# One attention kernel: the slope added by accumulating DMAs, the bar in one instruction, the mask in halves

## The chip, the cores and the metric

The kernel runs on one core of one Trainium2 chip. The metric is the device time of one execution in microseconds (us). The engines are named as the profile names them: PE (matrix multiply), PEld (its weight loads), DVE (the vector engine), ACT (the scalar engine), POOL (GpSimd) and SP (the sync engine, which issues DMAs). SBUF is the on-chip memory of 128 partitions, PSUM the memory that PE writes.

## The reference, cut to what matters

The input is 32 images of 32 channels and 56 x 56 = 3136 points. A locally connected 3 x 3 layer comes first. The part that fills most of the time is graph attention among the 3136 points of one image:

```python
p = pts / max(norm(pts, axis=1), 1e-12)
dist = sq + (-2 p @ p.T) + sq.T
_, nn_idx = top_k(-dist, 16)
nbr = pts[nn_idx]
logits = leaky_relu(cat(e, e_n) @ W_att + b_att, negative_slope=0.1)
attn = softmax(logits, axis=2)
agg = sum(nbr * attn, axis=2)
y = cat(pts, agg) @ W_conv + b_conv
```

A batch norm over y, a ReLU and a residual end it.

## The kernel before, in words

`build` (L1306) calls six stages; `attend` (L652) holds the change. It takes an image as 25 tiles of 128 query points (TILES), 800 tiles in all, and never gathers neighbours: it scores each query against all 3136 points, sets the logits of points outside the top 16 far below the rest, takes the exponential of all of them and sums with a matrix product.

Each engine runs its own stream; `each_step` (L638) calls a `body` for every step, in which `tile(0)` is the step's tile, `tile(-1)` the next one and `tile(1)` the one before. The order of calls in a body is the order on that engine; semaphores join the streams. The first and last steps are written out, and 50 steps (two images) are the body of a loop. What one tile goes through:

- PE `score` (L863): two halves of 1568 scores into PSUM. ACT `copy_scores` (L985, copy at L990) brings each half to `scores`, which has two buffers; the copy of quad 0 waits until the mask of the tile two steps back has read that buffer.
- ACT `rise` (L977, L982) writes the upper part of the leaky ReLU, relu(0.9 x logit) up to a factor, into `masked`, a ring of five buffers.
- POOL `add_slope` (L833, L843) adds the lower part, the slope (`shares`, one row for each image, in all partitions), to the first 1568 columns of `masked`, in two instructions of 784 columns. It is called for `tile(0)`, after the bar of `tile(1)`; the second instruction waits for the count of `tile(0)`.
- DVE `search` (L1084, L1088): the 8 largest of each 224 scores, 14 instructions. `merge` (L1144): from these the 16th largest, in a chain of six small instructions of which each waits on the semaphore `chain` for the one before (L1149 to L1159); the last, the count (L1159), raises `doubt_ready`.
- PE `add_doubts` (L878, L882) sums the counts, and DVE `settle_doubts` (L1096) loads the sum. If it isn't zero, five long instructions (L1102 to L1109) search the tile again.
- DVE `bar` (L1115): scores less the bound, capped at 0, for the first 1568 columns (L1118); the other 1568 are capped at `shares` instead (L1119), so the slope of these columns comes in here.
- DVE `mask` (L1122, L1127), one step later: adds `scores` to `masked`, and takes the smallest of the negated sums, in one instruction over 3136 columns. It raises `masked_ready`.
- ACT `exponentiate` (L1000, L1002): the exponential of `masked` and its total.
- PE `turn` (L884, L896 and L898) transposes `masked` in 25 blocks through two PSUM banks, ACT `copy_turned` (L1011, L1017) brings them back in 7 copies, and PE `aggregate` (L909, L916) multiplies. DVE `invert_total` (L1130) and `normalise` (L1134) scale the result, and a last product makes y.

SP's stream loads a batch's points, scores' second halves and shares ahead (`next_batch`, L791, in the step of tile 7 of the batch before), and loads and stores 64 KB pieces every fourth step. POOL's stream in `attend` is `add_slope` alone.

Of the kernel before, what the change touches and what calls it, by code (L numbers as in the profile page):

```python
# [5 lines left out]
FP32 = mybir.dt.float32  # L6
# [645 lines left out]
def attend(nc, feat, unit, pieces, share, table, W_emb, b_emb, W_att, b_att, W_conv, b_conv, y):  # L652
# [11 lines left out]
    POOL_COLS = N // 2  # L664
# [12 lines left out]
    with ExitStack() as stack:  # L677
# [14 lines left out]
        weight8 = enter(nc.sbuf_tensor("weight8", [P, PARTS, H8], FP32))  # L692
        best = enter(nc.sbuf_tensor("best", [P, NEIGHBOURS], FP32))
# [34 lines left out]
        logits_ready = enter(nc.semaphore("a_logits"))  # L728
# [3 lines left out]
        barred = enter(nc.semaphore("a_barred"))  # L732
        masked_ready = enter(nc.semaphore("a_masked"))
# [13 lines left out]
        y_stored1 = enter(nc.semaphore("a_y_stored1"))  # L747
        sp_passed = enter(nc.semaphore("a_sp_passed"))
# [5 lines left out]
        batch_in, feat_in, y_stored = [batch0, batch1], [feat0, feat1], [y_stored0, y_stored1]  # L754

# [71 lines left out]
        @block.gpsimd  # L827
        def _(pool):
            pool.wait_ge(cleared, 6)
            nc.gpsimd.affine_select(out=ident[:], in_=ident[:], compare_op=ALU.not_equal, fill=1.0, base=0,  # L830
                                    pattern=[[-1, P]], channel_multiplier=1).then_inc(ident_ready, 1)

            def add_slope(t, passed):  # L833

                pool.wait_ge(rises_ready, t.count(1, 1))
                if passed is not None:
                    pool.wait_ge(barred, passed.count(1, 1))
                width = POOL_COLS // 2
                for k in range(2):
                    if k == 1:  # L840
                        pool.wait_ge(doubt_ready, t.count(1, 1))
                    m = masked[:, t.ring, k * width:(k + 1) * width]
                    nc.gpsimd.tensor_tensor(m, m, shares[:, t.half, k * width:(k + 1) * width], ALU.add).then_inc(logits_ready, 1)  # L843

            def body(tile):
                if tile(0):
                    add_slope(tile(0), tile(1))

            each_step(pool, body)
# [113 lines left out]
        def _(act):  # L963
# [21 lines left out]
            def copy_scores(t, quad, used):  # L985

                act.wait_ge(scored, t.count(SCORED, SCORED_FREE + PER * (quad + 1)))
                if used is not None:
                    act.wait_ge(masked_ready, used.count(1, MASKED_FREE + 1))
                nc.scalar.activation(scores[:, t.par, quad * QUAD:(quad + 1) * QUAD].rearrange("p (a b) -> p a b", b=SCH),  # L990
                                     ps[:, 0:PER * BANK].rearrange("p (a b) -> p a b", b=BANK)[:, :, 0:SCH],
                                     ACT.Copy).then_inc(scores_in, 1)
# [27 lines left out]
            def body(tile):  # L1020
# [16 lines left out]
                if coming:  # L1037
                    copy_scores(coming, 1, None)
# [12 lines left out]
        def _(dve):  # L1051
# [63 lines left out]
            def bar(t):  # L1115

                low, high = scores[:, t.par, 0:POOL_COLS], scores[:, t.par, POOL_COLS:N]
                step(nc.vector.tensor_scalar(low, low, bound[:, 0:1], 0.0, ALU.subtract, ALU.min))  # L1118
                nc.vector.scalar_tensor_tensor(high, high, bound[:, 0:1], shares[:, t.half, POOL_COLS:N],  # L1119
                                               ALU.subtract, ALU.min).then_inc(barred, 1)  # L1120

            def mask(t):  # L1122

                gate(dve, logits_ready, t.count(2, 2), dve_passed)
                gate(dve, barred, t.count(1, 1), dve_passed)
                m = masked[:, t.ring, :]
                nc.vector.tensor_tensor_reduce(m, m, scores[:, t.par, :], -1.0, -NEVER, ALU.add, ALU.min,  # L1127
                                               minus_top[:, t.ring:t.ring + 1]).then_inc(masked_ready, 1)
# [15 lines left out]
            def merge(t, n):  # L1144

                found_all = found[:, t.par, :, :].rearrange("p a b -> p (a b)")
                last = best[:, NEIGHBOURS - 1:NEIGHBOURS]
                dve.wait_ge(chain, n)
                n = step(nc.vector.max(best[:, 0:H8], found_all))  # L1149
                dve.wait_ge(chain, n)  # L1150
                n = step(nc.vector.match_replace(rest[:], best[:, 0:H8], found_all, NEVER))
                dve.wait_ge(chain, n)
                n = step(nc.vector.max(best[:, H8:NEIGHBOURS], rest[:]))
                dve.wait_ge(chain, n)
                n = step(nc.vector.scalar_tensor_tensor(bound_low[:], over[:], last, margin[:], ALU.mult, ALU.subtract))
                dve.wait_ge(chain, n)
                n = step(nc.vector.scalar_tensor_tensor(bound[:], under[:], last, bound_low[:], ALU.mult, ALU.min))
# [187 lines left out]
```

## Time and profile before

| | |
|---|---|
| median of 3 runs | 11979.92 us (11979.1 to 11986.17) |
| span of the profiled execution | 11977.8 us, 2.1 us under that median |
| `attend`, tile by tile | from about 1.5 ms to 11.85 ms of the span |
| busy share of the span | DVE 86%, ACT 85%, PE 74%, POOL 27% |

The page of the profile gives the profiled execution's span and no other time of its own, so durations are set against the span. The span is the time from the first to the last instruction. A busy share is a mean over the whole span, so it mixes stages; views with a window show one stage. A group of instructions has one source line; its row gives its count, its busy time, the mean of one, and the idle time of its engine just before it with what ended it. "issue" is time in which an engine waited for nothing that the profile shows.

### The profile page before, as it was taken

The page shows a single profiled execution, that of the slowest core. Times are in us where ns is not written, and L with a number is a line of the kernel's source. Part 1 is how long each engine was busy: PE and PEld are TensorE (multiplying, and loading weights), DVE is VectorE, ACT ScalarE, POOL GpSimd, SP SyncE. Part 2 cuts the span into 40 slices and gives each one's busy share as a digit, 9 for nine tenths or more (in the row PEclk, how much of TensorE's full clock was granted, in tenths as well). Part 3 has the DMA queues.
Part 4 walks back from the last instruction along what each step waited for, and adds up shares of the span by engine and source line. Part 5 has one row for each costly group of instructions (what it writes and reads, how often), then busy time and mean ns, then how long its engine had stood idle before and what let it go on. Part 6 is the DMA issues. An engine that isn't in the chain of part 4 may idle for free. (4 is left out here: it accounts for less than half of the span.)

```text
span 11977.8 us, 322272 instructions
## 1 busy us (share of the span) xinstructions
PE 8919.8 (74%) x114746; PEld 6368.8 (53%) x114746; DVE 10276.0 (86%) x23897; ACT 10163.3 (85%) x11576; POOL 3199.6 (27%) x2040
## 2 busy tenths in 40 slices
PE   2885667777777777877777777777777777777775
PEld 2664345555555555555555555555555555545553
DVE  1000599999999999999999999999999999999997
ACT  2332489999999999999999998999999999989986
POOL 0221022222222222222222222222222222222221
PEclk9887889999999999999999999999999999999998
DMA  9666800000000000000000000000000000000003
GB/s 164 172 177 175 256 16 17 17 17 16 17 17 17 17 17 16 5 17 17 17 17 16 17 17 16 16 17 16 17 17 4 17 17 17 17 16 16 17 4 132
DMA packets 267542, 480.57 MB, mean 40 GB/s; under 512 B 196964, under 2 KB 197348, under 8 KB 248356
## 3 DMA queue, kind: packets, MB, share of 16 engines
q1 hardware_dynamic: 242532, 349.99, 12.5%
q0 software_dynamic: 23424, 109.21, 2.9%
q8 instruction: 1022, 16.74, 0.6%
q14 instruction: 564, 4.62, 0.1%
HBM read 353.59 MB, written 105.50 MB: 38 GB/s over the span
## 5 line engine op out<-in xcount | busy, mean ns | idle before, releaser
L843 POOL TENSOR_TENSOR masked<-masked,shares_a 128x784 f32<-128x784 f32 x1600 | 2988.8, 1868 | 7371.9 <-DVE rest L1159 4237.3
L1088 DVE MAX8 found<-scores 128x8 f32<-128x224 f32 x11200 | 3479.0, 370 | 223.7 <-ACT scores L990 188.9
L1017 ACT ACTIVATE turned_sb<-psum 128x512 f32<-128x512 f32 (+1 forms) x5600 | 2945.5, 572 | 507.7 <-PE psum L896 431.4
L898 PE MATMUL psum<-ident_a,masked 128*128 128x128 f32 x19200 | 2649.4, 282 | 902.8 <-ACT turned_sb L1017 860.9
L898 PEld LDWEIGHTS psum<-ident_a,masked 128*128 128x128 f32 x19200 | 2373.5, 195 | 1359.9 <-issue 1359.5
L1127 DVE CUSTOM_DVE_ANT_0 masked<-masked,scores 128x3136 f32<-128x3136 f32 x800 | 2719.1, 3399 | 0.2 <-DVE scores L1119 0.2
L990 ACT ACTIVATE scores<-psum 128x1568 f32<-128x1568 f32 x1600 | 2375.1, 1484 | 224.7 <-DVE minus_top L1127 190.0
L1002 ACT ACTIVATE masked<-masked,minus_top 128x3136 f32<-128x3136 f32 x800 | 2363.5, 2954 | 0.0
L982 ACT ACTIVATE masked<-shares_a,own 128x3136 f32<-128x3136 f32 x800 | 2328.4, 2910 | 1.0
L896 PE MATMUL psum<-ident_a,masked 128*128 128x128 f32 (+1 forms) x10400 | 1764.5, 284 | 528.7 <-ACT turned_sb L1017 494.1
L896 PEld LDWEIGHTS psum<-ident_a,masked 128*128 128x128 f32 (+1 forms) x10400 | 1106.7, 139 | 1289.1 <-issue 1213.3
L871 PE MATMUL psum<-points 32*128 32x392 f32 x12800 | 1542.1, 552 | 28.3 <-DMA rows<-table 16.4
L916 PE MATMUL psum<-turned_sb,rows 128*32 128x128 f32 (+1 forms) x40000 | 1554.9, 284 | 0.5 <-ACT inverse_sb L998 0.5
L1119 DVE SCALAR_TENSOR_TENSOR scores<-scores,bound,shares_a 128x1568 f32<-128x1568 f32 x800 | 1467.5, 1834 | 0.0
L916 PEld LDWEIGHTS psum<-turned_sb,rows 128*32 128x32 f32 (+1 forms) x40000 | 1159.1, 113 | 274.0 <-issue 176.5
L295 ACT ACTIVATE w_turned<-w_ps 96x384 f32<-96x384 f32 x784 | 347.2, 486 | 592.0 <-PE w_ps L254 588.4
L882 PE MATMUL psum<-ones,above 128*1 128x1 f32 x1600 | 150.8, 163 | 924.5 <-DVE rest L1159 924.5
L307 DVE COPY conv_sb<-conv_ps 128x128 f32 x196 | 57.1, 291 | 900.9 <-PE conv_ps L276 900.9
L1118 DVE TENSOR_SCALAR scores<-scores,bound 128x1568 f32<-128x1568 f32 x800 | 807.8, 1010 | 8.1 <-DVE bound L1109 2.5
L882 PEld LDWEIGHTS psum<-ones,above 128*1 128x1 f32 x1600 | 84.8, 80 | 1183.3 <-issue 1180.1
L871 PEld LDWEIGHTS psum<-points 32*128 32x128 f32 x12800 | 508.9, 186 | 229.3 <-issue 43.3
L254 PE MATMUL w_ps<-ident_c,w_in 128*96 128x128 f32 x2352 | 398.2, 312 | 232.6 <-DMA w_in<-in_L_conv_weight_dram 204.3
(137 smaller groups left out, 6415.4 us busy)
## 6 DMA issues: line engine op xcount, KB each, us to landing
w_in<-in_L_conv_weight_dram POOLq DMA_DIRECT2D x392, 144.0 KB, 3.4
w_in<-in_L_conv_weight_dram SPq DMA_DIRECT2D x392, 144.0 KB, 3.5
points<-unit SPq DMA_DIRECT2D x128, 392.0 KB
shares_a<-share SPq DMA_DIRECT2D x32, 1568.0 KB
windows<-xg SPq DMA_DIRECT2D x42, 928.0 KB, 13.5
xg<-padded SPq DMA_DIRECT2D x32, 406.0 KB, 16.8
table<-table_sb SPq DMA_DIRECT2D x32, 404.2 KB
rows<-table SPq DMA_DIRECT2D x32, 396.0 KB
```

The lines of the kernel that those rows point to most:

```text
L843: nc.gpsimd.tensor_tensor(m, m, shares[:, t.half, k * width:(k + 1) * width], ALU.add).then_inc(logits_ready, 1)
L871: nc.tensor.matmul(ps[:, r * BANK:r * BANK + SCH], points[C * r:C * (r + 1), t.half, t.queries()], points[C * r:C * (r + 1), t.half, at:at ...
L896: last = nc.tensor.transpose(out, block, ident[:])
L898: last = nc.tensor.matmul(out, block, ident[:], start=True, stop=True)
L916: last = nc.tensor.matmul(ps[q:q + C, SUM_BANK:SUM_BANK + P], rows[0:width, t.half, j, 0:C], turned_sb[0:width, t.par, j, :], start=j < PE ...
L982: nc.scalar.activation(masked[:, t.ring, :], shares[:, t.half, :], ACT.Relu, bias=own[:, t.half, at:at + 1], scale=STEEP / SLOPE).then_inc ...
L990: nc.scalar.activation(scores[:, t.par, quad * QUAD:(quad + 1) * QUAD].rearrange("p (a b) -> p a b", b=SCH), ps[:, 0:PER * BANK].rearrange ...
L1002: nc.scalar.activation(masked[:, t.ring, :], masked[:, t.ring, :], ACT.Exp, bias=minus_top[:, t.ring:t.ring + 1], scale=-1.0, accum_out=to ...
L1017: nc.scalar.activation(turned_sb[0:high, t.par, g * GROUP:g * GROUP + width // P, :].rearrange("p a b -> p (a b)"), ps[0:high, bank:bank + ...
L1088: n = step(nc.vector.max(found[:, t.par, c, :], scores[:, t.par, c * PART:(c + 1) * PART]))
L1119: nc.vector.scalar_tensor_tensor(high, high, bound[:, 0:1], shares[:, t.half, POOL_COLS:N], ALU.subtract, ALU.min).then_inc(barred, 1)
L1127: nc.vector.tensor_tensor_reduce(m, m, scores[:, t.par, :], -1.0, -NEVER, ALU.add, ALU.min, minus_top[:, t.ring:t.ring + 1]).then_inc(mask ...
```

## The change

The slope of all 3136 columns is added to `masked` by two DMAs that accumulate into SBUF, issued by GpSimd for `tile(-1)` as soon as its rise is written. The bar is then one instruction over all columns. The mask is two instructions of 1568 columns, the second starting from the first one's minimum; ACT's copy of quad 0 waits for the low half, that of quad 1 for the high half. The merge is taken apart, and its steps stand between the mask halves, `normalise` and `invert_total`.

```diff
@@ -661,7 +661,7 @@
     PART = 224
     PARTS = N // PART
     EARLY = PARTS // 2
-    POOL_COLS = N // 2
+    HALF = N // 2
     GROUP = 4
     T_GROUPS = -(-TILES // GROUP)
...
@@ -830,21 +835,16 @@
             nc.gpsimd.affine_select(out=ident[:], in_=ident[:], compare_op=ALU.not_equal, fill=1.0, base=0,
                                     pattern=[[-1, P]], channel_multiplier=1).then_inc(ident_ready, 1)
 
-            def add_slope(t, passed):
-
-                pool.wait_ge(rises_ready, t.count(1, 1))
-                if passed is not None:
-                    pool.wait_ge(barred, passed.count(1, 1))
-                width = POOL_COLS // 2
+            def add_slope(t):
+
+                gate(pool, rises_ready, t.count(1, 1), pool_passed)
                 for k in range(2):
-                    if k == 1:
-                        pool.wait_ge(doubt_ready, t.count(1, 1))
-                    m = masked[:, t.ring, k * width:(k + 1) * width]
-                    nc.gpsimd.tensor_tensor(m, m, shares[:, t.half, k * width:(k + 1) * width], ALU.add).then_inc(logits_ready, 1)
+                    cols = slice(k * HALF, (k + 1) * HALF)
+                    pool.dma_start(masked[:, t.ring, cols], shares[:, t.half, cols], accum_op=ALU.add).then_inc(slope_in[t.par], 16)
 
             def body(tile):
-                if tile(0):
-                    add_slope(tile(0), tile(1))
+                if tile(-1):
+                    add_slope(tile(-1))
 
             each_step(pool, body)
 
@@ -986,7 +986,10 @@
 
                 act.wait_ge(scored, t.count(SCORED, SCORED_FREE + PER * (quad + 1)))
                 if used is not None:
-                    act.wait_ge(masked_ready, used.count(1, MASKED_FREE + 1))
+                    if quad == 0:
+                        act.wait_ge(low_masked, used.count(1, 1))
+                    else:
+                        act.wait_ge(masked_ready, used.count(1, MASKED_FREE + 1))
                 nc.scalar.activation(scores[:, t.par, quad * QUAD:(quad + 1) * QUAD].rearrange("p (a b) -> p a b", b=SCH),
                                      ps[:, 0:PER * BANK].rearrange("p (a b) -> p a b", b=BANK)[:, :, 0:SCH],
                                      ACT.Copy).then_inc(scores_in, 1)
@@ -1035,7 +1038,7 @@
                 if older:
                     copy_inverse(older, tile(SUM_LAG + 1))
                 if coming:
-                    copy_scores(coming, 1, None)
+                    copy_scores(coming, 1, tile(1))
                 if past:
                     copy_turned(past, 2)
                     copy_turned(past, 3)
@@ -1114,18 +1117,23 @@
 
             def bar(t):
 
-                low, high = scores[:, t.par, 0:POOL_COLS], scores[:, t.par, POOL_COLS:N]
-                step(nc.vector.tensor_scalar(low, low, bound[:, 0:1], 0.0, ALU.subtract, ALU.min))
-                nc.vector.scalar_tensor_tensor(high, high, bound[:, 0:1], shares[:, t.half, POOL_COLS:N],
-                                               ALU.subtract, ALU.min).then_inc(barred, 1)
-
-            def mask(t):
-
-                gate(dve, logits_ready, t.count(2, 2), dve_passed)
+                s = scores[:, t.par, :]
+                nc.vector.tensor_scalar(s, s, bound[:, 0:1], 0.0, ALU.subtract, ALU.min).then_inc(barred, 1)
+
+            def mask_low(t):
+
+                gate(dve, slope_in[t.par], t.same_par(32, 32), dve_passed)
                 gate(dve, barred, t.count(1, 1), dve_passed)
-                m = masked[:, t.ring, :]
-                nc.vector.tensor_tensor_reduce(m, m, scores[:, t.par, :], -1.0, -NEVER, ALU.add, ALU.min,
-                                               minus_top[:, t.ring:t.ring + 1]).then_inc(masked_ready, 1)
+                m = masked[:, t.ring, 0:HALF]
+                nc.vector.tensor_tensor_reduce(m, m, scores[:, t.par, 0:HALF], -1.0, -NEVER, ALU.add, ALU.min,
+                                               low_top[:, t.par:t.par + 1]).then_inc(low_masked, 1)
+
+            def mask_high(t):
+
+                gate(dve, low_masked, t.count(1, 1), dve_passed)
+                m = masked[:, t.ring, HALF:N]
+                nc.vector.tensor_tensor_reduce(m, m, scores[:, t.par, HALF:N], -1.0, low_top[:, t.par:t.par + 1],
+                                               ALU.add, ALU.min, minus_top[:, t.ring:t.ring + 1]).then_inc(masked_ready, 1)
 
             def invert_total(t):
                 dve.wait_ge(exp_ready, t.count(1, 1))
@@ -1141,36 +1149,64 @@
                 nc.vector.tensor_tensor(agg[:, t.group_par, at:at + P], ps[:, SUM_BANK:SUM_BANK + P], inverse_sb[:],
                                         ALU.mult).then_inc(agg_ready, 1)
 
-            def merge(t, n):
...
+            def top_first(t, n):
+
+                dve.wait_ge(chain, n)
+                return step(nc.vector.max(best[:, 0:H8], found_of(t)))
...
+            def count_above(t, n):
+
                 dve.wait_ge(chain, n)
-                nc.vector.scalar_tensor_tensor(rest[:], found_all, bound[:, 1:2], weight8[:].rearrange("p a b -> p (a b)"),
+                nc.vector.scalar_tensor_tensor(rest[:], found_of(t), bound[:, 1:2], weight8[:].rearrange("p a b -> p (a b)"),
                                                ALU.is_ge, ALU.mult, accum_out=above[:, 0:1]).then_inc(doubt_ready, 1)
 
             def body(tile):
-                here, coming = tile(0), tile(-1)
+                here, coming, passed = tile(0), tile(-1), tile(1)
                 if here:
                     n = search(here, 1)
-                if tile(1):
-                    mask(tile(1))
+                if passed:
+                    mask_low(passed)
                 if here:
-                    merge(here, n)
+                    n = top_first(here, n)
+                if passed:
+                    mask_high(passed)
+                if here:
+                    n = drop_first(here, n)
                 if tile(NORM_LAG):
                     normalise(tile(NORM_LAG))
+                if here:
+                    n = top_second(n)
                 if tile(3):
                     invert_total(tile(3))
+                if here:
+                    n = lower_bound(n)
+                    n = set_bound(n)
+                    count_above(here, n)
                 if coming:
                     search(coming, 0, 0, 2)
                 if here:
```

The parts left out in the last hunk are `drop_first`, `top_second`, `lower_bound` and `set_bound`: the other steps of `merge`, each with its own wait on `chain`, their instructions unchanged.

## Rows read from the trace of the kernel before

**Rows 1.** The page of the profile: its span and each engine's busy time.

```profile
span 11977.8 us, 322272 instructions
...
PE 8919.8 (74%) x114746; PEld 6368.8 (53%) x114746; DVE 10276.0 (86%) x23897; ACT 10163.3 (85%) x11576; POOL 3199.6 (27%) x2040
```

**Rows 2.** Windows, 5000 to 6000 us: busy by engine, clock, DMA share, GB/s.

```profile
5000.00:6000.00 1000.00, 774.66 (x9054) 547.38 (x9058) 963.32 (x2268) 938.30 (x1042) 291.58 (x156) 0.98 0.07 15
```

**Rows 3.** Waits by engine, 2000 to 11800 us: total us, times, longest.

```profile
ACT turned_sb L1017 <- PE psum L896: 407.3, 653, 2.2
...
ACT scores L990 <- DVE minus_top L1127: 167.1, 14, 12.4
...
DVE found L1088 <- ACT scores L990: 161.1, 340, 4.6
...
PE psum L882 <- DVE rest L1159: 855.6, 546, 14.2
```

**Rows 4.** Timeline, a settled step: start us, us, engine, line, operation.

```profile
5650.22 2.96 ACT L1002 ACTIVATE masked<-masked,minus_top 128x3136 f32<-128x3136 f32 x1
...
5651.69 3.39 DVE L1127 CUSTOM_DVE_ANT_0 masked<-masked,scores 128x3136 f32<-128x3136 f32 x1
...
5655.13 0.60 ACT L1017 ACTIVATE turned_sb<-psum 128x512 f32<-128x512 f32 x1 [0.65 <-PE psum L896]
...
5655.62 1.47 ACT L990 ACTIVATE scores<-psum 128x1568 f32<-128x1568 f32 x1
...
5656.52 0.34 DVE L1159 SCALAR_TENSOR_TENSOR rest<-found,bound,weight 128x112 f32<-128x112 f32 x1
...
5657.16 0.19 PE L882 MATMUL psum<-ones,above 128*1 128x1 f32 x2 [1.25 <-DVE rest L1159]
...
5658.95 0.35 PE L875 MATMUL psum<-halves_a,minus 3*128 3x392 bf16 x4
...
5660.41 1.50 ACT L990 ACTIVATE scores<-psum 128x1568 f32<-128x1568 f32 x1
...
5662.07 2.14 DVE L1088 MAX8 found<-scores 128x8 f32<-128x224 f32 x7
...
5662.73 2.96 ACT L1002 ACTIVATE masked<-masked,minus_top 128x3136 f32<-128x3136 f32 x1
```

**Rows 5.** Groups of DVE instructions: xcount, busy us, mean ns, idle before.

```profile
L1127 DVE CUSTOM_DVE_ANT_0 masked<-masked,scores 128x3136 f32<-128x3136 f32 x800 | 2719.1, 3399 | 0.2 <-DVE scores L1119 0.2
L1119 DVE SCALAR_TENSOR_TENSOR scores<-scores,bound,shares_a 128x1568 f32<-128x1568 f32 x800 | 1467.5, 1834 | 0.0
L1118 DVE TENSOR_SCALAR scores<-scores,bound 128x1568 f32<-128x1568 f32 x800 | 807.8, 1010 | 8.1 <-DVE bound L1109 2.5 <-DVEq L1111 1.2
...
L1108 DVE TENSOR_SCALAR scores<-scores 128x3136 f32<-128x3136 f32 x15 | 26.9, 1793 | 0.5
...
L1157 DVE SCALAR_TENSOR_TENSOR bound<-under,best,bound_low 128x2 f32<-128x2 f32 x800 | 176.5, 221 | 28.2
```

**Rows 6.** Timeline, a step with doubts: its two ACT copies of scores.

```profile
3038.67 1.48 ACT L990 ACTIVATE scores<-psum 128x1568 f32<-128x1568 f32 x1 [11.81 <-DVE minus_top L1127]
...
3044.52 1.48 ACT L990 ACTIVATE scores<-psum 128x1568 f32<-128x1568 f32 x1 [0.92 <-PE psum L875]
```

**Rows 7.** Timeline beside a batch load: a rise, and that tile's mask.

```profile
2847.47 2.91 ACT L982 ACTIVATE masked<-shares_a,own 128x3136 f32<-128x3136 f32 x1
...
2867.47 3.41 DVE L1127 CUSTOM_DVE_ANT_0 masked<-masked,scores 128x3136 f32<-128x3136 f32 x1
```

**Rows 8.** DMA queues, 0 to 12 us: packets, MB, share of 16 engines.

```profile
q0 software_dynamic: 288, 3.21, 67.7%
```

**Rows 9.** Tile x_in: issue ns min/median/max, and its landing.

```profile
L78 POOL DMA_DIRECT2D x_in<-in_x_dram x8: 527/527/674, 1.8 to 116.0; - x8
...
DMA to landing us min/median/max: 6.7/12.3/16.0
```

**Rows 10.** Windows, during one batch load.

```profile
2847.00:2864.00 17.00, 12.27 (x137) 8.59 (x138) 16.67 (x45) 16.56 (x19) 5.60 (x3) 0.94 0.97 216
```

More of the change, by code:

```diff
@@ L692, in attend @@
         weight8 = enter(nc.sbuf_tensor("weight8", [P, PARTS, H8], FP32))
+        low_top = enter(nc.sbuf_tensor("low_top", [P, 2], FP32))
         best = enter(nc.sbuf_tensor("best", [P, NEIGHBOURS], FP32))
@@ L727, in attend @@
         rises_ready = enter(nc.semaphore("a_rises"))
-        logits_ready = enter(nc.semaphore("a_logits"))
+        slope0 = enter(nc.semaphore("a_slope0"))
+        slope1 = enter(nc.semaphore("a_slope1"))
         doubt_ready = enter(nc.semaphore("a_doubt"))
@@ L732, in attend @@
         barred = enter(nc.semaphore("a_barred"))
+        low_masked = enter(nc.semaphore("a_low_masked"))
         masked_ready = enter(nc.semaphore("a_masked"))
@@ L747, in attend @@
         y_stored1 = enter(nc.semaphore("a_y_stored1"))
+        pool_passed = enter(nc.semaphore("a_pool_passed"))
         sp_passed = enter(nc.semaphore("a_sp_passed"))
@@ L754, in attend @@
         batch_in, feat_in, y_stored = [batch0, batch1], [feat0, feat1], [y_stored0, y_stored1]
+        slope_in = [slope0, slope1]
         SCORED_FREE, SUMMED_FREE, MASKED_FREE, Y_FREE, FEAT_FREE = 1, 1, 1, 1, 2
@@ L1142, in normalise, with found_of @@
                                         ALU.mult).then_inc(agg_ready, 1)
-            def merge(t, n):
-                found_all = found[:, t.par, :, :].rearrange("p a b -> p (a b)")
-                last = best[:, NEIGHBOURS - 1:NEIGHBOURS]
+            last = best[:, NEIGHBOURS - 1:NEIGHBOURS]
+            def found_of(t):
+                return found[:, t.par, :, :].rearrange("p a b -> p (a b)")
+            def top_first(t, n):
                 dve.wait_ge(chain, n)
-                n = step(nc.vector.max(best[:, 0:H8], found_all))
+                return step(nc.vector.max(best[:, 0:H8], found_of(t)))
@@ L1150, in merge, with drop_first, top_second, lower_bound @@
+            def drop_first(t, n):
                 dve.wait_ge(chain, n)
-                n = step(nc.vector.match_replace(rest[:], best[:, 0:H8], found_all, NEVER))
+                return step(nc.vector.match_replace(rest[:], best[:, 0:H8], found_of(t), NEVER))
+            def top_second(n):
                 dve.wait_ge(chain, n)
-                n = step(nc.vector.max(best[:, H8:NEIGHBOURS], rest[:]))
+                return step(nc.vector.max(best[:, H8:NEIGHBOURS], rest[:]))
+            def lower_bound(n):
@@ L1154, in merge, with set_bound @@
                 dve.wait_ge(chain, n)
-                n = step(nc.vector.scalar_tensor_tensor(bound_low[:], over[:], last, margin[:], ALU.mult, ALU.subtract))
+                return step(nc.vector.scalar_tensor_tensor(bound_low[:], over[:], last, margin[:], ALU.mult, ALU.subtract))
+            def set_bound(n):
                 dve.wait_ge(chain, n)
-                n = step(nc.vector.scalar_tensor_tensor(bound[:], under[:], last, bound_low[:], ALU.mult, ALU.min))
+                return step(nc.vector.scalar_tensor_tensor(bound[:], under[:], last, bound_low[:], ALU.mult, ALU.min))
```

## The prediction

> **What bounds the kernel now.** I read the busy shares first, then the waits, then one step in order of time. DVE is busy 10276 us and ACT 10163 us of a span of 11977.8 us [rows 1]; inside the attention stage DVE has 963 and ACT 938 us of every 1000 [rows 2]. By shares alone DVE would be the bound. The waits say otherwise. Over 9800 us, ACT waits for DVE 14 times, 11.9 us each, 167 us in all; DVE waits for ACT 340 times [rows 3]. So outside 14 stalls ACT never stands still for DVE. The stalls are the steps in which `settle_doubts` takes its long branch; L1108, which only that branch issues, ran 15 times [rows 5].
>
> The settled step shows the pace. The exp of one step starts at 5650.22 and that of the next at 5662.73: 12.51 us. Between them ACT has one gap, 0.65 us before L1017, and what ends it is PE, whose transposes wait in turn for ACT's earlier copies out of PSUM [rows 4]. DVE's mask ends at 5651.69 + 3.39 = 5655.08, and the copy of scores that it frees starts only at 5655.62, behind another ACT copy. At the other half of the step DVE's search starts at 5662.07, just behind the end of the ACT copy that feeds it (5660.41 + 1.50 = 5661.91). PE has 1.1 us to spare: it waits 1.25 us for the count (L1159), its scores are done at 5658.95 + 0.35 = 5659.30, and ACT takes them at 5660.41. A step is ACT's own work plus a PE gap that this change does not touch, with DVE almost as long.
>
> **The change part by part.**
> - *Bar.* Two instructions, 1.010 + 1.834 us, become one over 3136 columns; L1108 is that operation at that size, 1.793 us [rows 5]: -1.05 us of DVE a step.
> - *Mask in halves.* 3.399 us for 3136 columns becomes two of 1568. L1118 and L1108 give the fixed part of a DVE instruction on this shape: 2 x 1.010 - 1.793 = 0.23 us [rows 5]. The cost lies between 0 and 0.23; I take +0.2, since each half also reads its own accumulator. The low half frees the first score copy some 1.6 us earlier.
> - *Interleaved merge.* L1157 is one of five merge steps that each wait for the one before; 28.2 us over 800 is 0.035 us a time [rows 5]. Three of them get other work in front: -0.1 us. With that, DVE is 0.95 us a step shorter. The count (L1159) comes later in the chain, though: half-masks 0.2, the normalise and the reciprocal now ahead of it some 0.2, less 0.1 of gaps, so +0.3 us. PE's 1.1 us covers it; without that cover ACT's second score copy would slip by 0.3 us a step, 240 us.
> - *GpSimd's adds* go, and nothing that ACT or PE does waits for them.
> - *The DMAs.* Per step, two of 128 x 1568 floats, 1.606 MB together. GpSimd issues them when the rise ends, about 0.53 us each [rows 9], and has nothing else queued behind them. On the same queue two copies of 1.606 MB took 0.677 x 12 = 8.1 us of ring time, so 4.06 us for a step's bytes [rows 8]; the quickest landing was 6.7 us from issue, that is 2.6 us around the ring time [rows 9]. The trace has no accumulating DMA. From below it costs a copy, 4.06 us a pair, and not less, as the same bytes are written. The adder has two operands to read, which gives 8.1 us; I take that. From above the only row is x_in's worst landing, 16.0 us, with other transfers beside it.
> - *The new wait.* `mask_low` waits for both DMAs. Behind it on DVE stands everything: merge, search, bar; behind those PE's doubts and both ACT score copies. But a rise that ends at 2847.47 + 2.91 = 2850.38 has its mask at 2867.47, 17.1 us later [rows 7], and two issues + 2.6 + 8.1 are 11.8 us. The rings are 0.07 busy now [rows 2] and would be some 0.7 busy. SP's queue shares them: its small loads and stores are used steps later.
> - *ACT's second score copy* now waits for the high half, over 4 us before ACT gets there.
>
> At one place a row can be set against a rule. The bar runs 3136 columns in 1.793 us, where the mask takes 3.399 [rows 5], so it moves about two elements in the time of one. The Trainium skill (SBUF — State Buffer, Who interferes with whom) says that DVE in such a two-port mode locks GpSimd out for the whole instruction, and that descriptors for GpSimd's DMAs are written through that port. By it an issue at the rise's end can wait out the bar, 1.8 us more, and the landing comes 13.6 us after the rise, still inside 17.1; no row here shows it.
>
> **The sum.** In plain steps: nothing, since ACT sets 12.5 us and does not wait for DVE. DVE's 0.95 us becomes waiting for ACT's scores. In the 15 steps with doubts ACT stalls twice [rows 6]: 11.81 us for the mask, then 0.92 for PE's scores, which wait for the count. The first stall shrinks by 1.05 + 1.6 = 2.65. The second is set by the count, which comes only 1.05 - 0.3 = 0.75 us earlier, so most of the 2.65 is waited out there. 15 x 0.75 = 11 us; bounds 0 and 15 x 2.65 = 40. From the profiled execution's 11978: **11967 us**; the median of the runs is 2 us above that span, so 11969.
>
> **The rivals.**
> - *The batch load delays the DMAs: slower.* While a batch's points and shares load, the rings are 0.97 busy for 17 us at 216 GB/s [rows 10], and a rise ends some 3 us into it [rows 7]. If the pair gets half of each ring, 8.1 us becomes 16.2; with 2.6 and the issues that is 19.9 us against 17.1, and the mask is late by about 2.8 us, less some 0.5 us of slack. Of 32 batches one is loaded ahead of the stage: 31 x 2 is some +60 us, up to 31 x 2.8 = +87 if the slack doesn't count: about **12030**. It decides once the pair needs more than (17.1 - 3.7)/2 = 6.7 us of ring by itself; a plain copy's 4.06 would stay clear. For it: x_in's median landing was 12.3 us where the best was 6.7 [rows 9]. Against it: the load may leave room that the pair can fill. That the ring time doubles is also what the Trainium skill says (Collectives: The Full Stack, The bandwidth ceiling): the add costs nothing itself, but two source reads halve the rate. No accumulating transfer is in this trace.
> - *The rings become the bound: much slower.* Past 12.5 us of ring per pair, three times a copy, every step grows. At x_in's worst, 16.0 us, 3.5 x 800 = +2800 us: 14770. Nothing but the lack of a row speaks for it.
> - *Faster.* If the first stall alone counted in steps with doubts, -40: 11940. If DVE set the pace after all, 0.95 x 800 = -760: 11220; the 14 waits of ACT speak against it, the busy shares for it.
>
> **How the numbers follow.** A measurement of this kernel tells about 0.2%, 24 us, from no change. No effect in plain steps: 0.50. Batch loads: 0.26. Ring-bound: 0.13. Faster: 0.11, of which 0.07 around 11940 and 0.04 DVE-paced. So faster 0.11, same 0.50, slower 0.39. The range leaves out the ring-bound and the DVE-paced case: from 11935 (all 40 us of the doubts, and 5 for mask halves that cost nothing) to 12070: the load's +87, and 14 for late counts in steps where PE has less to spare.
>
> **What would show it.** Right: exps 12.5 us apart as before, the 0.65 us gap still there, DVE's busy time near 0.95 x 800 = 760 us lower and its waits for ACT's scores up by about as much; ACT's stalls for the mask shorter by 2.65 us with a longer one for PE behind. The batch-load rival: DVE waits for slope DMAs once or twice a batch. The ring-bound one: that wait in every step and a DMA share near 1. I am wrong if steps come closer than 12.5 us, or if ACT's operations change their length with the DMAs beside them.

## The result, and the profile after

The changed kernel takes 12183.1 us (median of 4 runs, 12168.62 to 12183.79) where the kernel before, run beside it, takes 11979.51: a ratio of 1.0168 [1.0154, 1.0183], slower by 204 us. 11969 us was forecast, and the range ended at 12070.

The page of the changed kernel, its span, busy times and DMA queues (queue: packets, MB, share of 16 engines):

```profile
span 12180.7 us, 325029 instructions
...
PE 8975.9 (74%) x114746; PEld 6412.3 (53%) x114746; DVE 9588.0 (79%) x24697; ACT 10173.5 (84%) x11576; POOL 1729.2 (14%) x2040
...
q0 software_dynamic: 253824, 1393.82, 56.0%
q1 hardware_dynamic: 242532, 349.99, 12.1%
q8 instruction: 1023, 16.76, 0.6%
```

Against [rows 1], DVE is 688 us less busy, 0.86 us a step, and ACT as busy as before; the span grew all the same. GpSimd's queue q0 is the new item. The window of [rows 2] shows the same in the middle of the stage, with a DMA share of 0.68 where it was 0.07:

```profile
5000.00:6000.00 1000.00, 773.74 (x8882) 546.31 (x8880) 875.77 (x2292) 918.91 (x1019) 145.61 (x154) 0.96 0.68 138
```

The waits of the changed kernel, 2000 to 11900 us (total us, times, longest):

```profile
PE psum L882 <- DVE rest L1185: 1001.6, 549, 13.7
DVE found L1091 <- ACT scores L993: 927.2, 1393, 7.6
...
ACT turned_sb L1020 <- PE psum L896: 410.8, 654, 2.1
...
ACT scores L993 <- DVE low_top L1128: 193.9, 42, 10.1
...
DVE masked L1128 <- DMA masked<-shares_a: 121.9, 28, 5.0
ACT turned_sb L1020 <- PE psum L898: 116.9, 73, 7.9
PE psum L898 <- issue: 94.0, 14, 7.5
```

Three things are to be seen beside [rows 3]. DVE's wait for ACT's scores grew from 161.1 to 927.2 us while ACT's own gap behind L896 stayed (407.3, now 410.8): the time that DVE saved became waiting. DVE waits for the slope DMAs 28 times in this window, 4.4 us each; ACT's waits for the mask rose from 14 to 42, so those 28 reach ACT. And PE stands still 14 times for "issue", up to 7.5 us; the kernel before had 12 such waits in 2000 to 11800 us, the longest 4.4 us:

```profile
PE psum L898 <- issue: 40.5, 12, 4.4
```

To place the loss I took the starts of all exponentials from the two traces and set each of the 799 steps against 12.5 us (the median step is 12.50 us in both). The sums of what is over, in us:

| | 15 steps with doubts | the step in which the loop of 50 turns | all others | together |
|---|---|---|---|---|
| before | 196.9 | 67.3 | 66.8 | 331.0 |
| after | 186.1 | 127.2 | 217.5 | 530.7 |
| difference | -10.8 | +59.9 | +150.7 | +199.7 |

The loop's body runs 15 times, so it turns back 14 times. Of the 217.5, 152.2 lie in one step of each image, behind the batch load: 29 of these take 16.9 to 18.5 us. The other 3 us of the span lie ahead of the first exponential.

**A batch load** in the changed kernel, in order of time:

```profile
2867.37 0.95 SPq L786 DMA_DIRECT2D points<-unit  x1
...
2868.10 2.91 ACT L982 ACTIVATE masked<-shares_a,own 128x3136 f32<-128x3136 f32 x1
...
2871.58 1.77 POOL L843 DMA_DIRECT2D masked<-shares_a  x2 [10.74 <-ACT masked L982]
...
2872.28 27.80 SPq L792 DMA_DIRECT2D rows<-table  x1
...
2886.34 2.96 ACT L1005 ACTIVATE masked<-masked,minus_top 128x3136 f32<-128x3136 f32 x1
...
2892.23 1.79 DVE L1128 CUSTOM_DVE_ANT_0 masked<-masked,scores 128x1568 f32<-128x1568 f32 x1 [4.40 <-DMA masked<-shares_a]
...
2894.13 1.48 ACT L993 ACTIVATE scores<-psum 128x1568 f32<-128x1568 f32 x1 [2.28 <-DVE low_top L1128]
...
2897.90 0.19 PE L882 MATMUL psum<-ones,above 128*1 128x1 f32 x2 [5.87 <-DVE rest L1185]
```

The rise ends at 2871.01, the pair is issued by 2873.35, and the low mask that waits for it starts at 2892.23, 18.9 us after the second issue. Merge, count and bar stand behind that mask on DVE; PE waits 5.87 us for the count, and the next exponential comes at 2904.14, 17.80 us after the one at 2886.34. The load suffers as well: its long issue took 13.56 us in the kernel before and takes 27.80 here.

Meanwhile the queues (packets, MB, share of 16 engines; packets overlap, so a share can pass 100%) show in 2873.4 to 2877.9, in 2878 to 2885 and in 2885.5 to 2892, in this order:

```profile
q1 hardware_dynamic: 117, 0.98, 108.4%
```

```profile
q1 hardware_dynamic: 107, 1.22, 52.5%
q0 software_dynamic: 102, 0.64, 46.9%
```

```profile
q0 software_dynamic: 232, 1.25, 94.3%
```

So the pair doesn't share the rings with the load from the start. Its first packet moves 7.0 us after its first issue, where the median of all pairs is 1.44; then the two queues have about half each, and then the pair has the rings nearly alone. Why the load's packets go first is not shown.

**A turn of the loop**, the very next step of the same kernel:

```profile
2904.14 2.91 ACT L1005 ACTIVATE masked<-masked,minus_top 128x3136 f32<-128x3136 f32 x1
2906.09 0.66 PE L896 MATMUL psum<-ident_a,masked 128*128 128x128 f32 x4
2906.23 2.15 DVE L1091 MAX8 found<-scores 128x8 f32<-128x224 f32 x7 [4.73 <-issue]
...
2913.32 2.05 PE L898 MATMUL psum<-ident_a,masked 128*128 128x128 f32 x8 [6.57 <-issue]
...
2915.40 0.60 ACT L1020 ACTIVATE turned_sb<-psum 128x512 f32<-128x512 f32 x1 [7.77 <-PE psum L898]
```

and the same turn in the kernel before:

```profile
2884.48 1.13 PE L898 MATMUL psum<-ident_a,masked 128*128 128x128 f32 x8 [1.89 <-issue]
2885.65 0.60 ACT L1017 ACTIVATE turned_sb<-psum 128x512 f32<-128x512 f32 x1 [2.39 <-PE psum L898]
```

At this turn PE has nothing to execute for 6.57 us instead of 1.89, and ACT waits 7.77 us instead of 2.39 for what PE makes. The turn shown of the kernel before is one of its shorter ones: by the waits above, the mean went from 40.5/12 = 3.4 us to 94.0/14 = 6.7. Nothing that the profile shows releases PE there; what it lacks has to be found by experiment.

### The profile page after: what moved, and what is told of

It reads as the page before. It is cut to its first block and busy times, and to the rows that moved or that the text cites. A ratio compares the mean times of both kernels' runs of the same rounds, so it can differ in the third digit from the quotient of the medians.

```text
span 12180.7 us, 325029 instructions
## 1 busy us (share of the span) xinstructions
PE 8975.9 (74%) x114746; PEld 6412.3 (53%) x114746; DVE 9588.0 (79%) x24697; ACT 10173.5 (84%) x11576; POOL 1729.2 (14%) x2040
## 3 DMA queue, kind: packets, MB, share of 16 engines
q1 hardware_dynamic: 242532, 349.99, 12.1%
## 5 line engine op out<-in xcount | busy, mean ns | idle before, releaser
L898 PE MATMUL psum<-ident_a,masked 128*128 128x128 f32 x19200 | 2678.4, 284 | 886.2 <-ACT turned_sb L1020 790.9
L843 POOL DMA_DIRECT2D masked<-shares_a x1600 | 1518.4, 986 | 9037.4 <-ACT masked L982 8683.9
L896 PE MATMUL psum<-ident_a,masked 128*128 128x128 f32 (+1 forms) x10400 | 1766.5, 285 | 523.6 <-ACT turned_sb L1020 485.3
L896 PEld LDWEIGHTS psum<-ident_a,masked 128*128 128x128 f32 (+1 forms) x10400 | 1109.0, 140 | 1276.8 <-issue 1204.7
L1128 DVE CUSTOM_DVE_ANT_0 masked<-masked,scores 128x1568 f32<-128x1568 f32 x800 | 1418.8, 1773 | 131.7 <-DMA masked<-shares_a 131.5
L1135 DVE CUSTOM_DVE_ANT_0 masked<-masked,scores,low_top 128x1568 f32<-128x1568 f32 x800 | 1480.4, 1850 | 5.7 <-issue 5.6
L1121 DVE TENSOR_SCALAR scores<-scores,bound 128x3136 f32<-128x3136 f32 x800 | 1462.9, 1829 | 11.4 <-DVE bound L1112 2.8
L875 PE MATMUL psum<-halves_a,minus 3*128 3x392 bf16 x6400 | 569.2, 335 | 0.0
```

The costliest lines, as they stand in the source:

```text
L843: pool.dma_start(masked[:, t.ring, cols], shares[:, t.half, cols], accum_op=ALU.add).then_inc(slope_in[t.par], 16)
L896: last = nc.tensor.transpose(out, block, ident[:])
L898: last = nc.tensor.matmul(out, block, ident[:], start=True, stop=True)
L1121: nc.vector.tensor_scalar(s, s, bound[:, 0:1], 0.0, ALU.subtract, ALU.min).then_inc(barred, 1)
L1135: nc.vector.tensor_tensor_reduce(m, m, scores[:, t.par, HALF:N], -1.0, low_top[:, t.par:t.par + 1], ALU.add, ALU.min, minus_top[:, t.ring: ...
```

## The experiments

The theory: the accumulating DMAs hold the rings twice as long as a copy, and two things then come late, the pair that meets a batch load, and at the loop's turn the code that PE needs next. Its rivals: the turn is longer because the load stretches into it; the add has no part in it, and any DMA of this size would cost the same; DVE's new order loses by itself. The last runs ask whether DVE's saved time can be turned into a gain.

Each ratio is against the kernel before, run on the same chip. The table splits each profiled execution as above (us over 12.5 a step), so that a row can be read beside each experiment:

| | doubts | loop turns | all others |
|---|---|---|---|
| before | 196.9 | 67.3 | 66.8 |
| after | 186.1 | 127.2 | 217.5 |
| load_spread | 185.9 | 117.9 | 73.3 |
| load_late | 185.4 | 116.4 | 234.3 |
| before_load_late | 196.6 | 51.8 | 97.0 |
| slope_copy | 186.6 | 97.2 | 96.3 |
| spread_four | 185.2 | 88.4 | 61.4 |
| half_dma | 200.3 | 113.9 | 204.4 |
| dve_only | 199.6 | 73.6 | 126.9 |

**load_spread.** The batch load is cut in seven pieces, one in each step of tiles 10 to 16, so that it doesn't fill the rings at a stretch.

```diff
-                if here and here.c == 7 and not (isinstance(here.i, int) and here.at > ALL - TILES):
+                if here and FIRST <= here.c < FIRST + len(PIECE) and not (isinstance(here.i, int) and here.at >= ALL - TILES):
                     next_batch(here)
...
+            def next_batch(t):
+                k = t.c - FIRST
...
+                gate(sp, masked_ready, t.count(1, 0), sp_passed)
+                PIECE[k](t.batch(1, 1), 1 - t.half)
```

> The changed kernel with the batch load cut into seven pieces, one per step in the steps of tiles 10 to 16, each behind a mask. Theory (slope DMAs share the rings with the batch load and land late): DVE's 122 us of waits for the slope DMAs go, and with them the 5 us that the step after each of the 31 loads loses, 150 us: 12183 - 150 = 12030 us. If the dear loop turn (22 us in the changed kernel against 17 before) is an after-effect of that load, it falls back too: 11965. Rival (the DMAs slow every step a little): stays at 12180.

12007.71 us, 1.0041 [1.0027, 1.0055]. The wait for the slope DMAs is gone from the list of waits, the longest landing fell from 20.2 to 13.0 us, and "all others" came back to 73.3. So the batch load against the slope DMAs is some 144 us of the loss (217.5 less 73.3). The turns stay long: `PE psum L912 <- issue` is 95.1 us in 14 times, as after. The colliding load is not what lengthens them.

**load_late** moves the whole load from the step of tile 7 to that of tile 14, so that the turn and the load lie apart; **before_load_late** does the same in the kernel before.

```diff
-                if here and here.c == 7 and not (isinstance(here.i, int) and here.at > ALL - TILES):
+                if here and here.c == 14 and not (isinstance(here.i, int) and here.at > ALL - TILES):
```

> The changed kernel with the whole batch load moved from the step of tile 7 to that of tile 14, away from the turn of the loop, which comes in the step of tile 8 of every second image. Theory: the collision with the slope DMAs stays, 31 x 5 us, now at tile 14. Theory A of the turn (instructions are fetched behind slope DMAs whenever they are in the rings): turns stay near 22 us, total 12180. Theory B (only the load made the turn dear): turns fall to 17 us or under, 15 x 4.5 = 70 us less, 12110.

> The kernel before with the batch load moved in the same way. Its turns take 16.5 to 18 us with the load close by. If the load is part of that, turns fall to some 15 us and the total by up to 35 us, to 11945; if not, 11980.

load_late: 12157.26 us, 1.016 [1.0143, 1.0177]. The lost steps moved with the load, and DVE's wait for the slope stayed; its row of the waits, 2000 to 11500 us:

```profile
DVE masked L1128 <- DMA masked<-shares_a: 109.4, 27, 4.8
```

The turns, now far from any load, are still 20.5 to 21.4 us. before_load_late: 11965.82 us, 1.0004 [0.9994, 1.0013], with turns of 15.1 to 17.6 us. By the table the load adds some 0.8 us (after) to 1.1 us (before) to each of the 14 turns, and the slope DMAs add (116.4 - 51.8)/14 = 4.6.

**slope_copy.** The slope DMAs copy and don't accumulate. The logits then lack the rise, but the bytes written and the waits are those of the change.

```diff
-                    pool.dma_start(masked[:, t.ring, cols], shares[:, t.half, cols], accum_op=ALU.add).then_inc(slope_in[t.par], 16)
+                    pool.dma_start(masked[:, t.ring, cols], shares[:, t.half, cols]).then_inc(slope_in[t.par], 16)
```

> The changed kernel with the accumulation left out: the two DMAs copy the slope over the rise, so the logits lack it (the rise is lost) while every instruction and wait stays. Theory (reading two operands doubles the ring time, and that alone makes the pair late): ring time of a pair falls from 8.0 to 4.0 us, the waits for slope DMAs fall from 28 to about 0, 150 us go, and the turns get cheaper by about half of their extra: 11990 to 12000 us. Rival (the pair is late because of its issue on GpSimd or its queueing, whatever it moves): waits and 12180 us stay.

12012.17 us, 1.0046 [1.0032, 1.006]. Its page, its landings (us, min/median/max) and its wait:

```profile
q0 software_dynamic: 253824, 1393.82, 29.4%
```

```profile
DMA to landing us min/median/max: 3.5/5.5/16.5
```

```profile
DVE masked L1128 <- DMA masked<-shares_a: 15.0, 20, 1.4
```

With the 2.9% of q0 that other stages use taken off, a pair of copies holds the rings for (0.294 x 12010 - 347)/800 = 3.98 us, and the accumulating pair for (0.560 x 12181 - 347)/800 = 8.09 us. At half the ring time the steps behind the batch loads lose 19 us in place of 152, and the turns half as much as in after (97.2 where before has 67.3). Beside a load the first packet of the copies comes as late as that of the adds, 6.8 to 7.5 us after the issue, so it is the shorter ring time that saves the deadline. Both losses go with the time for which a slope DMA holds the rings.

**spread_four.** load_spread, with the same bytes in four DMAs of 784 columns.

```diff
-                for k in range(2):
-                    cols = slice(k * HALF, (k + 1) * HALF)
+                width = HALF // 2
+                for k in range(4):
+                    cols = slice(k * width, (k + 1) * width)
...
-                gate(dve, slope_in[t.par], t.same_par(32, 32), dve_passed)
+                gate(dve, slope_in[t.par], t.same_par(64, 64), dve_passed)
```

> load_spread with four slope DMAs of 784 columns a tile in place of two of 1568. At the loop's turn the first fetch of instructions starts 3.7 us after PE's branch there, against 0.1 to 0.8 before the change, just when the first of the two slope DMAs leaves the rings. Theory (a fetch waits for the slope DMA in flight, not for all that is queued): fetches start some 2 us earlier, turns fall from 20.8 to about 19, 15 x 2 = 30 us: 11980. Rival (it waits for all queued transfers, or it does not depend on them): turns stay at 20.8 or more, 12008 or above; two more issues on GpSimd a step are 1.8 us and covered.

11971.19 us, 1.0000 [0.999, 1.001]: as fast as the kernel before. The turns still cost 21 us more, and the doubts 12 and the plain steps 5 us less. The turn can be watched in the DMA view, whose queue q8 brings instructions. The exponential at the turn starts at 2862.29 us in load_spread and at 2860.90 in spread_four. The queues of load_spread in 2862.0 to 2865.5, and then in 2865.5 to 2866.5:

```profile
q0 software_dynamic: 131, 0.74, 108.9%
```

```profile
q0 software_dynamic: 31, 0.18, 87.6%
q8 instruction: 2, 0.03, 21.6%
```

and of spread_four in 2860.9 to 2862.4, and then in 2862.4 to 2863.4:

```profile
q0 software_dynamic: 98, 0.26, 101.2%
```

```profile
q0 software_dynamic: 57, 0.18, 96.7%
q8 instruction: 2, 0.03, 18.2%
```

The kernel before has its turn's exponential at 2879.72; in 2879.7 to 2880.7 it has the first packet of q8 already:

```profile
q8 instruction: 1, 0.02, 8.4%
```

In load_spread no instruction packet moves for over 3.2 us while slope packets fill the rings, and two move as soon as the first slope DMA has left; with DMAs of half the size they move after 1.5 to 2.5 us. All 14 turns of each trace say the same: the first packet of q8 starts 0.1 to 1.4 us behind the turn's exponential in the kernel before, 3.7 to 4.1 in load_spread and 1.4 to 2.1 in spread_four, and in 40 of these 42 turns PE goes on 4.3 to 4.8 us behind that packet. So PE's wait follows the fetch: here 65.9 us in 14 times where load_spread had 95.1, and the turns are 18.7 to 19.4 us for most, where they were 20.7 to 21.3. The fetch of the code behind the branch queues behind the slope DMA in flight.

**half_dma** sends only the low half by a DMA and puts the high half's slope in the bar as before; **dve_only** has no slope DMA at all (GpSimd's adds and the two bars of before, with DVE's new order). They should show what DVE's part does alone.

```diff
-                for k in range(2):
+                for k in range(1):
...
-                s = scores[:, t.par, :]
-                nc.vector.tensor_scalar(s, s, bound[:, 0:1], 0.0, ALU.subtract, ALU.min).then_inc(barred, 1)
+                low, high = scores[:, t.par, 0:HALF], scores[:, t.par, HALF:N]
+                step(nc.vector.tensor_scalar(low, low, bound[:, 0:1], 0.0, ALU.subtract, ALU.min))
+                nc.vector.scalar_tensor_tensor(high, high, bound[:, 0:1], shares[:, t.half, HALF:N],
+                                               ALU.subtract, ALU.min).then_inc(barred, 1)
```

> The changed kernel with one accumulating DMA a tile, for the low 1568 columns; the slope of the other half comes in through the bar on DVE again, in two instructions as before. Theory: 4 us of ring a step is clear of the 6.7 us that the deadline leaves, so no waits for the slope DMA and no 150 us; the loop turns cost some 2 to 4 us more than before each, 30 to 60 us; DVE is 0.1 us a step longer than before: 11990 to 12030 us. Rival (any accumulating DMA beside the load makes DVE wait): over 12080.

> The kernel before with only DVE's new order: mask in halves, merge steps between, GpSimd's adds and the bar in two instructions as before, no DMA. Theory (all of the loss is the DMAs' doing, and DVE does not set the pace): within 0.3% of the kernel before, loop turns at 16 to 18 us. Rival (the later count or the halved mask cost time): 12040 or more, with ACT waiting for PE's scores.

half_dma: 12139.33 us, 1.0133 [1.0116, 1.015], a miss by over 100 us. The slope waits shrank to 7.1 us in all and the fetch still waits for one DMA (turns about 20.6 us), as expected. But "all others" is 204.4: many plain steps take 13.1 to 13.8 us, with PE at 1.2 in place of 2.4 GHz for part of them. By the trace's clock records from 1.6 ms on, PE is at the lower level for 1350 us, where it was 675 in the kernel before and 920 in after; the mean granted clock is 0.926, after's 0.943. dve_only: 12029.83 us, 1.0045 [1.0028, 1.0062], clock 0.944, a smaller miss of the same kind. So the new order on DVE, without the shorter bar, is itself a loss. The suspect was the later count, which keeps PE waiting.

**half_dma_count** tries that: the count goes ahead of the high half of the mask.

```diff
                 if here:
                     n = top_first(here, n)
-                if passed:
-                    mask_high(passed)
...
                     count_above(here, n)
+                if passed:
+                    mask_high(passed)
```

> half_dma lost 1.3% though it waits for no slope DMA: many of its steps took 13.1 to 13.8 us with PE at the lower of its two clock levels, and PE stood idle up to 1.7 us for the count in them. This is half_dma with the count ahead of the high half of the mask, so 1.8 us earlier. Theory (the later count leaves PE idle longer, its clock falls, and the transposes hold ACT up): the mean granted clock rises from 0.926 to 0.95 and the time falls from 12139 to about 12010 us. Rival (one DMA a step costs that much in another way): it stays at 12139.

12227.79 us, 1.0214 [1.0197, 1.0231], clock 0.900: worse. Its waits, 2000 to 11800 us, and then half_dma's:

```profile
PE psum L898 <- ACT turned_sb L1020: 1303.9, 735, 2.7
...
PE psum L882 <- DVE rest L1187: 143.6, 24, 12.6
```

```profile
PE psum L882 <- DVE rest L1187: 852.6, 495, 14.3
PE psum L898 <- ACT turned_sb L1020: 725.4, 708, 2.7
```

PE hardly waits for the count any more. The idle time came back as one longer wait for ACT, and the clock fell further. A late count alone doesn't explain half_dma's clock; why it drops stays open.

**spread_reorder** and **before_reorder** test whether DVE's spare time can be used: ACT's copy of score quad 0 moves ahead of the first copy out of PE's transposes, in load_spread and in the kernel before.

```diff
+                if coming:
+                    copy_scores(coming, 0, tile(1))
                 if past:
                     copy_turned(past, 0, tile(5))
                 if coming:
-                    copy_scores(coming, 0, tile(1))
```

> load_spread with one call of ACT's body moved: the copy of score quad 0 ahead of the first copy of transposes, so that it fills ACT's 0.65 us gap. The low half of the mask is ready early enough for it. Theory (ACT's own work and that gap set the step, and DVE has 0.95 us to spare): 0.65 us less in the three of four steps that have the gap, 0.75 x 0.65 x 780 = 380 us: 11630. Rival (DVE, or the chain from its count through PE to ACT's second copy, holds the step): above 11850.

> The kernel before with the same call moved. There the whole mask ends 0.5 us before ACT's copy now starts, so the copy moved up would wait for it. Theory (DVE is almost as long as ACT, so ACT alone can gain little): 11880 to 11980 us. Rival (ACT's order alone was the bound, and DVE has time): 11630, as in the run beside it.

spread_reorder: 11599.88 us, 0.9686 [0.967, 0.9702], with steps of 11.7, 12.1 and 12.5 us. before_reorder: 11964.16 us, 0.9991 [0.9981, 1.0001]; its waits, 2000 to 11800 us, show why:

```profile
ACT scores L990 <- DVE minus_top L1128: 540.5, 692, 13.2
```

In the kernel before ACT then meets a mask that isn't done. In spread_reorder, 2000 to 11500 us, such a wait is left in the steps with doubts alone:

```profile
ACT scores L1007 <- DVE low_top L1143: 148.6, 14, 11.0
```

The low half of the mask frees the buffer early enough. The spread load itself was not tried in the kernel before, but the steps behind its loads are only 5.7 us over in all, so little can be won there. ACT's gap behind PE, which had set the pace, can be closed only together with the change.

**spread_reorder_count** adds half_dma_count's early count to that, and **all_four** adds spread_four's DMAs and moves the copy of y from ACT to DVE.

```diff
-                if tile(COPY_LAG) and tile(COPY_LAG).ends_group():
-                    copy_y(tile(COPY_LAG))
...
+                nc.vector.tensor_copy(y_sb[Y0:Y0 + C, t.group_par, 0:width], ps[Y0:Y0 + C, Y_BANK:Y_BANK + width]).then_inc(y_in, 1)
```

> spread_reorder with the count ahead of the high half of the mask in the same way. Its steps go 11.73, 11.72, 12.11, 12.45: in the third PE makes y first and its scores are late for ACT, in the fourth ACT copies y. Theory (an earlier count gives PE the time for y): 12.11 falls to 11.8, 0.3 x 200 = 60 us: 11540. Rival (ACT is full and PE's lateness costs nothing): 11600.

> spread_reorder_count with the four smaller slope DMAs, and the copy of y out of PSUM moved from ACT to DVE, which has time for it. Theory (ACT's own work is the bound of the step; the turns shrink as in spread_four): the step with the copy of y falls from 12.46 to about 11.87, 0.59 x 200 = 118 us, the turns by 15 x 2 = 30: 11561 - 148 = 11410. Rival (DVE's waits for ACT's scores were no time to spare, since they come where the copy can't stand): 11530.

spread_reorder_count: 11560.85 us, 0.9659 [0.9643, 0.9675]. The plain steps did not get shorter, against what was expected; 24 of the 31 us that its profiled steps gained lie in the 15 steps with doubts (25.1 us each before, 23.5 now). all_four: 11472.29 us, **0.9581 [0.9565, 0.9597]**, the fastest of the study; most steps take 11.72 us. It stays short of its expectation; one step in each image now takes 12.9 to 14.5 us. Its waits, 2000 to 11300 us:

```profile
ACT scores L1008 <- PE psum L890: 101.4, 206, 1.8
PE psum L944 <- DVE y_sb L1099: 76.7, 30, 14.3
```

PE holds its product for y back until DVE has copied the last one, late in DVE's step, and ACT's scores wait behind PE.

## Why the prediction was wrong, step by step

- *ACT sets 12.5 us, and DVE's saving turns into waiting*: right. The median step is 12.50 us in both kernels, ACT's gap behind L896 is unchanged, and DVE's waits for scores rose by 766 us, where 760 were forecast.
- *DVE's parts*: right within 0.1 us a step. After's groups (count, busy us, mean ns):

```profile
L843 POOL DMA_DIRECT2D masked<-shares_a x1600 | 1518.4, 986 | 9037.4 <-ACT masked L982 8683.9
...
L1128 DVE CUSTOM_DVE_ANT_0 masked<-masked,scores 128x1568 f32<-128x1568 f32 x800 | 1418.8, 1773 | 131.7 <-DMA masked<-shares_a 131.5
L1135 DVE CUSTOM_DVE_ANT_0 masked<-masked,scores,low_top 128x1568 f32<-128x1568 f32 x800 | 1480.4, 1850 | 5.7 <-issue 5.6
L1121 DVE TENSOR_SCALAR scores<-scores,bound 128x3136 f32<-128x3136 f32 x800 | 1462.9, 1829 | 11.4 <-DVE bound L1112 2.8
```

  The halves are 1.773 + 1.850 = 3.623 against 3.399 [rows 5]: +0.22 for the +0.2 taken. The bar is 1.829 for 1.793.
- *Doubts*: right. 25.63 us a step became 24.90, -0.73 where -0.75 was forecast, some 11 us in all.
- *Ring time of a pair, 8.1 us*: right, 8.09 against 3.98 for copies. The Trainium skill's rule (Collectives: The Full Stack, The bandwidth ceiling), that an add halves the rate by its second read, agrees with both figures; that the second read is the reason is not shown by any run.
- *The batch load*: **the step that failed first.** It was a rival at 0.26, not a term of the sum; what spoke against it, that the load may leave room for the pair, does not hold: the load alone fills the rings (108.4% above), and 29 steps pay. Its size was too low as well, some 60 us where 150 were lost; by its own 2.8 less 0.5 us it would have been 31 x 2.3 = 71. The rival's 16.2 + 2.6 = 18.8 us from the second issue to the landing agrees with the 18.9 in the rows above, but that is luck: the pair didn't get half of the rings all along, it got nothing for 5.2 us after its second issue, then half, then nearly all. By the half share a copied pair would have stayed clear; in slope_copy DVE still waits for it 20 times, up to 1.4 us. Two smaller numbers failed. The issues were taken at 0.53 us each [rows 9]; one takes 0.99 us in the mean, and the first starts 0.57 us after the rise. And 0.5 us of slack was taken off, where there is none: DVE stands still 4.4 us, and the step loses 5.3 (17.80 less 12.50), since PE, ACT and the next count queue up behind that mask.
- *The loop turn*: **missing from the sum**, some +50 to +60 us. Where the DMAs were costed, only SP's loads and stores were named as sharing the rings. The queue that brings instructions shares them too, and PE can't go on without it.
- *The new order of merge and mask*: +0.3 us for a later count was said to be covered by PE's 1.1 us. In the changed kernel that holds: all its steps but those of the doubts, the turns and the loads have 65 us over, where before has 67. With the long bar, in dve_only and half_dma, steps grew, and half_dma_count shows that the late count isn't the whole reason.
- *The lock of GpSimd by the bar* (the Trainium skill, SBUF — State Buffer, Who interferes with whom): by it an issue can wait out a bar, 1.8 us. The trace agrees with the lock. A bar, and the one issue that starts in it (its ns as min/median/max, and its start):

```profile
2883.18 1.85 DVE L1121 TENSOR_SCALAR scores<-scores,bound 128x3136 f32<-128x3136 f32 x1
```

```profile
L843 POOL DMA_DIRECT2D masked<-shares_a x1: 1067/1067/1067, 2884.1 to 2884.1; - x1
```

  Of 1600 issues 739 start inside a bar and none ends before it. 267 of them still have 0.8 us or more of the bar ahead, and all but one end 0.12 to 0.15 us behind it. But it costs little: in the median 0.74 us of the bar are left when the issue starts, and an issue takes 0.865 us at least. So the 1.8 us more were an upper end; the median issue takes 0.913 us.

With both losses as terms, at the sizes of the table, the sum would have been 151 + 60 - 11 = +200 us.

## What to carry to other kernels

Work moved to DMAs is paid on the rings, so set its ring time beside every burst and every queue that shares them, the instruction fetch at a loop's turn included: cut a burst into pieces over the steps, and a long DMA into shorter ones, and the cost can go. Spare time on an engine that doesn't set the pace is worth nothing until the order on the engine that does is changed to use it: the reorder gave 0.1% alone, at the edge of what can be told, and over 3% together with the change.

## What the runs showed of the hardware

- A fetch of instructions waits for the slope DMA in flight. One DMA of 128 rows of 6272 bytes is 8 rows for each of the 16 engines and 8.09/2 = 4.05 us of ring time; with it the first packet of the fetch came 3.7 to 4.1 us behind the exponential in load_spread, with half the row size 1.4 to 2.1 in spread_four, and without any 0.1 to 1.4. The Trainium skill (DMA: Bandwidth & Descriptors, Queues, rings and completion order) has a DMA engine change queues only between packets, each of many descriptors; the trace agrees if the 8 rows make one such packet, which it doesn't show. The Trainium skill (Runtime: NRT & Kernel Launch, Instruction fetch mechanics) says that a taken branch out of the pages at hand waits for a DMA; PE's idle time at a turn, 3.4 us in the mean before and 6.7 after, agrees.
- A DMA of GpSimd's that meets a full load of SP's queue moves nothing at first: its first packet came 6.8 to 7.5 us after the issue in nearly all steps beside a load, as an add and as a copy, where the median is 1.4.
- The bar of 1.8 us on DVE holds back an issue on GpSimd until 0.12 to 0.15 us behind its end.
- An accumulating DMA costs GpSimd more to issue than a copy of the same shape: 0.865 us at least against 0.527 in slope_copy.
- Another order on DVE can go with a lower clock of PE, with DVE as busy as before: half_dma (DVE 10276 us, as in the kernel before) was granted 0.926 and dve_only 0.944, where the kernel before was granted 0.946 to 0.955 on the same chip. half_dma_count, in which PE's waits for the count are gone and those for ACT longer, was granted 0.900. What decides it is open.
